# Attention and a mixture of experts on one core: half of each tile's gated row is turned by a DMA transpose instead of on TensorE

## The reference, cut to what matters

```python
x = x + _layernorm(attn(_layernorm(x), wq, wk, wv, wo))
z = _layernorm(x)
for _ in range(LOOPS):
    z_norm = rmsnorm(z, norm_w)
    scores = softmax(z_norm @ router_w)
    topk_vals, topk_idx = top_k(scores, 2)
    for e in range(E):        
        h = silu(flat_z @ w1[e]) * (flat_z @ w3[e])
        mixed = mixed + flat_cw[:, e:e + 1] * (h @ w2[e])
    z = z + mixed
x = x + _layernorm(z)
```

## Time and profile before

| what | value |
|---|---|
| median of 3 runs | 1050.5 us (1049.72 to 1050.72) |
| profiled execution, its own time | 1050.72 us |
| span of the profile (first to last instruction) | 1049.0 us |
| TensorE busy | 987.4 us (94%) |
| VectorE, ScalarE, Pool busy | 690.5, 574.7, 579.5 us |
| queue q1 (SyncE's DMAs), share of the 16 DMA engines | 26.5% |
| queue q0 (Pool's DMAs) | 12.0% |

### The profile page before, as it was taken

How to read it: one execution, slowest core, us unless ns; L and a number is a source line. 1 busy time by engine, 2 the same in 40 slices (tenths; PEclk the granted TensorE clock), 3 DMA queues, 4 the chain that set the end, 5 groups by cost and what they waited for, 6 DMA issues and landing times.

```text
span 1049.0 us, 22711 instructions
## 1 busy us (share of the span) xinstructions
PE 987.4 (94%) x7246; PEld 678.7 (65%) x7246; DVE 690.5 (66%) x1497; ACT 574.7 (55%) x1122; POOL 579.5 (55%) x755
## 2 busy tenths in 40 slices
PE   7999997989999899999999999999999999999991
PEld 5677776668888577665666765666755566666661
DVE  7889987999999454684435557535469433575557
ACT  4578786668888545433335565335574333333333
POOL 3356686866798755444443366443365544455435
PEclk9999999999999999999999999999999999999996
DMA  9921111000000234334346435338434433665573
GB/s 315 370 68 31 38 32 22 1 6 21 15 26 16 67 107 125 87 69 101 91 109 167 132 98 139 88 106 181 112 111 117 96 91 92 170 173 119 143 187 130
DMA packets 153818, 109.26 MB, mean 104 GB/s; under 512 B 100992, under 2 KB 140544, under 8 KB 153728
## 3 DMA queue, kind: packets, MB, share of 16 engines
q1 hardware_dynamic: 140096, 70.82, 26.5%
q0 software_dynamic: 13632, 37.24, 12.0%
HBM read 54.27 MB, written 31.20 MB: 81 GB/s over the span
## 4 chain that ended last, share of the span: by engine, by line
PE 69%; DVE 9%; POOL 7%; DMA 6%; ACT 4%; issue 3%; SPq 0%; another core or an unknown queue 0%; POOLq 0%; ACTq 0%; DVEq 0%
PE psum_s L930 32%; PE psum_o L2336 16%; PE psum_s L2325 6%; DMA arena<-arena 4%; PE psum_s L1758 3%; PE psum_t L1753 2%; PE psum_t L764 2%; PE psum_o L1804 2%; POOL arena L1057 2%; DVE arena L1489 1%; DMA arena<-in_rope 1%; PE psum_o L1799 1%; PE psum_o L1811 1%; PE psum_s L1735 1%; PE psum_t L2300 1%
## 5 line engine op out<-in xcount | busy, mean ns | idle before, releaser
L930 PE MATMUL psum_s<-w_all,arena 128*128 x1704 | 392.0, 380 | 4.6 <-issue 1.9
L1980 POOL DMA_INDIRECT token_rows<-arena,result_row_of_row x142 | 147.1, 1036 | 296.5 <-ACT arena L2089 291.2
L930 PEld LDWEIGHTS psum_s<-w_all,arena 128*128 128x128 f16 x1704 | 157.8, 98 | 185.2 <-issue 10.9
L2336 PE MATMUL psum_o<-w_all,arena 128*128 x1704 | 209.4, 273 | 9.1 <-DVE arena L2264 8.2
L915 DVE SCALAR_TENSOR_TENSOR arena<-psum_s,gate_scale,arena 128x512 f32<-128x512 f32 x142 | 106.5, 750 | 161.1 <-ACT arena L909 80.6
L2336 PEld LDWEIGHTS psum_o<-w_all,arena 128*128 128x128 f16 x1704 | 164.7, 98 | 54.1 <-issue 15.4
L2264 DVE TENSOR_TENSOR arena<-psum_s,arena 128x512 f16<-128x512 f32 x142 | 97.8, 689 | 132.3 <-ACT arena L2082 114.2
L2089 ACT ACTIVATE arena<-psum_o 128x256 f32<-128x256 f32 x142 | 54.3, 383 | 216.8 <-PE psum_o L2336 214.1
L891 POOL DMA_INDIRECT arena<-sorted_rows,token_of_row x142 | 139.9, 986 | 49.3 <-issue 40.2
L909 ACT ACTIVATE arena<-psum_s,silu_scale 128x512 f32<-128x512 f32 x142 | 97.6, 687 | 108.1 <-PE psum_s L930 56.6
L2082 ACT ACTIVATE arena<-psum_s 128x512 f16<-128x512 f32 x142 | 84.7, 597 | 33.1 <-PE psum_s L2325 22.9
(11 more groups left out here) (326 smaller groups left out, 1364.8 us busy)
## 6 DMA issues: line engine op xcount, KB each, us to landing
arena<-token_rows SPq DMA_DIRECT2D x64, 256.0 KB, 3.1
w_all<-in_L_ffn_w SPq DMA_DIRECT2D x24, 512.0 KB, 10.1
sorted_rows<-w_all SPq DMA_DIRECT2D x24, 256.0 KB
out<-x_sb SPq DMA_DIRECT2D x7, 512.0 KB, 3.1
arena<-arena SPq DMA_TRANSPOSE x172, 2.4
arena<-sorted_rows,token_of_row POOLq DMA_INDIRECT x142
token_rows<-arena,result_row_of_row POOLq DMA_INDIRECT x142
x_sb<-in_L_attn_x SPq DMA_DIRECT2D x1, 2048.0 KB, 14.8
```

Source lines behind the costliest of these rows:

```text
L930: last = nc.tensor.matmul(bank, e_xT[:, u, lx * DC + c, :], w_split[:, bass.ds(e * EW + at, FF)], start=(q == 0), stop=(q == 3 * DC - 1))
L1980: nc.gpsimd.indirect_dma_start(rows, bass.IndirectOffsetOnAxis(ap=targets[:, at : at + 1], axis=0), y_row[:, u, :], None).then_inc(s_sent[ ...
L2336: last = nc.tensor.matmul(psum_e, hT[:, lh, c, :], w_split[:, bass.ds(e * EW + at, D)], start=(q == 0), stop=(q == 3 * FC - 1))
```

## The change

`h_row` is gated in two halves of 256 columns, the second one first. That half is split into 16-bit hi and lo as it stands: ScalarE rounds it (`half_hi`), VectorE writes the rest (`half_lo`), into `h_split`. One DMA transpose on SyncE turns both parts of it (`turn_half`) into `hT[1]`. TensorE turns the first half in two transposes instead of four; `h_hi` and `h_lo` work on 256 columns. `outer` reads blocks 0 and 1 from `hT[0]` and then waits for the DMA before blocks 2 and 3. The buffers for results go from three to two, which frees the room for `h_split`. On SyncE `turn_half(n)` stands first in turn n, `turn_rows` goes from two tiles ahead to three, and `store_rows` comes one turn later.

```diff
             dve.wait_ge(s_b, s + 1)
             dve.wait_ge(s_silu, s + 1)
-            nc.vector.scalar_tensor_tensor(h_row, psum_b, gate_scale[:, 0:1], silu_a, ALU.mult,
-                                           ALU.mult).then_inc(s_h, 1)
+            if s:
+                dve.wait_ge(s_half_lo, s)
+            for half, signal in ((slice(FF // 2, FF), s_gated), (slice(0, FF // 2), s_h)):
+                nc.vector.scalar_tensor_tensor(h_row[:, half], psum_b[:, half], gate_scale[:, 0:1], silu_a[:, half], ALU.mult,
+                                               ALU.mult).then_inc(signal, 1)
...
+            def turn_half(n):
+
+                sp.wait_ge(s_half_lo, n + 1)
+                if n:
+                    sp.wait_ge(s_e, n)
+                sp.dma_start(hT[1].rearrange("p l c t -> p (l c) t"), h_split.rearrange("p l c -> p (l c)"),
+                             transpose=True).then_inc(s_half_T, 16)
...
-                    turn_rows(sp, FIRST[k] + t + 2)
+                    n = FIRST[k] + t
+                    turn_half(n)
+                    if n == 0:
+                        turn_rows(sp, 2)
+                    turn_rows(sp, n + 3)
...
-                    if k < END and 0 <= t - plan.split - 1 < PAIRS:
-                        store_rows(k, t - plan.split - 1)
+                    if k < END and 0 <= t - plan.split - 2 < PAIRS:
+                        store_rows(k, t - plan.split - 2)
...
+            def half_hi(n):
+                act.wait_ge(s_gated, n + 1)
+                if n:
+                    act.wait_ge(s_half_T, 16 * n)
+                nc.scalar.activation(h_split[:, 0, :], h_row[:, FF // 2 :], ACT.Copy).then_inc(s_half_hi, 1)
 
             def y_copy(n):
-                u = n % UNROLL
                 act.wait_ge(s_e, n + 1)
-                if n >= UNROLL:
-                    act.wait_ge(s_sent[u], 16 * (n // UNROLL))
-                nc.scalar.activation(y_row[:, u, :], psum_e, ACT.Copy).then_inc(s_yrow, 1)
+                if n >= 2:
+                    act.wait_ge(s_sent[(n - 2) % UNROLL], 16 * ((n - 2) // UNROLL + 1))
+                nc.scalar.activation(y_row[:, n % 2, :], psum_e, ACT.Copy).then_inc(s_yrow, 1)
...
                     if k < END:
                         beside(k, plan, t)
+                    half_hi(n)
                     if n:
                         y_copy(n - 1)
...
+            def half_lo(n):
+                dve.wait_ge(s_half_hi, n + 1)
+                nc.vector.tensor_tensor(h_split[:, 1, :], h_row[:, FF // 2 :], h_split[:, 0, :], ALU.subtract).then_inc(s_half_lo, 1)
...
                     gate(dve, n)
+                    half_lo(n)
                     if k < END:
                         beside(k, plan, t)
...
-                for c in range(FC):
+                for c in range(FC // 2):
                     last = nc.tensor.transpose(psum_h[:, c * P : (c + 1) * P], h_row[:, c * P : (c + 1) * P], ident[:, :])
...
+                    if q == 3 * FC // 2:
+                        pe.wait_ge(s_half_T, 16 * (n + 1))
```

20 lines of the change are left out of this document (13 added, 7 removed).

## The result

The changed kernel takes **1152.1 us** (median of 4 runs, 1147.6 to 1154.3), the kernel before 1050.6 in the same series: a ratio of 1.096, 95% interval 1.092 to 1.100. The forecast was 1087 us, with a range of 1062 to 1112. The sign was right, the loss was 101.5 us and not 36.5.

What follows compares the result with a forecast made beforehand. TensorE's instruction stream was taken to bound the expert stage. 1050.7 - 21.8 (transposes) + 31.6 (store loop) + 13 (large loads) + 5 (last-pass loads) + 4.7 (VectorE) + 4 (small things) = 1087.2 us; range 1062 to 1112.

Steps and rivals of the forecast that it cites:

- What it no longer has to do is worth its full price: TensorE in the expert stage: two fewer transposes save 0.22 us in each of 99 tiles, -21.8 us.
- The price per transpose: TensorE: each further transpose costs 0.11 us, as transposes overlap, though one lasts 0.27 us.
- The paragraph on quiet tiles: Undisturbed tiles: VectorE's split gating ends in time for the transposes, hidden; 0.13 us per tile if uncovered.
- Slack 0.7 us: hidden in quiet tiles: Undisturbed tiles: the half's DMA transpose lands at 3.85 us after gate, needed at 4.58, so it costs nothing.
- Rival (c): Quiet tiles: transposes meeting gathers or scatters land late, each of 99 tiles loses 0.3 us, 1117 us; chance 0.13.
- The store loop: Row stores, first three passes: half, store landing and ScalarE's row writes wait on each other in a ring; +31.6 us.
- Large loads: Before tiles 42, 73, 113 and 137: the next half's transpose stands behind four 256 KB loads; 4 x 3.3 = +13 us.
- L930's and the outer product's matmuls as long as before: Expected sign in the profile after: these TensorE matmuls keep their duration, with transposes halved to some 43 us busy.
- Loads of the last pass: Tiles 115 to 120: load pairs issued behind both transposes keep VectorE waiting, +5 us; second and third pass just fit.
- VectorE and small things: Tiles where VectorE ends last, its side work starting later, +4.7 us; several effects under 2 us each, +4 us.
- (a): Rival: the half is always in time, also behind stores and loads; faster, 1034 us; chance 0.07.
- (b): Rival: stores don't bind but large loads do; 1056 us; chance 0.08.

Runs made afterwards that it cites:

- x3_two_turns_index: The kernel before with two of four TensorE transposes per tile left out and the next expert's number loaded ahead of the transposes; 1019.5 us, ratio 0.973.
- x9_own_half: The kernel with all four edits, but TensorE reads the first half's turned data twice and never waits for the second half's DMA; 1073.9 us, ratio 1.026.
- x11_half_unread: x9_own_half with the half's DMA reading constant weights; ScalarE's wait for its landing and SyncE's for the outer product removed; 1038.5 us, ratio 0.989.
- all four edits: Changed kernel with expert number loaded before transposes, stores issued earlier, large loads spread, ScalarE's half ahead of row writes in those tiles; 1072.6 us, ratio 1.022.
- x1_index_first: The changed kernel with TensorE loading the next tile's expert number ahead of the two transposes, not behind them; 1135.7 us, ratio 1.085.

## Why the prediction was wrong, by its own steps

**"What it no longer has to do is worth its full price"**: this is the step that failed, in the first paragraph. The earlier trace rows show a tile without a gap on TensorE, and the prediction took that for proof that only matmuls bound it. A second path through the same engine's queue, gate to expert number to address to first inner matmul, was 0.01 us shorter than the path through the transposes, and its instruction stands in the trace of before. The price per transpose, 0.11 us, was right (x3_two_turns_index: 4.12 for 4.35). The paragraph on quiet tiles priced the split gate at 0.13 us per tile "if that cover were gone". The transposes keep this cover, they start 1.11 behind the gate as before; the load of the number has none, and the tile is 0.12 longer. Instead of -0.22 per quiet tile the change brings +0.12: for 64 tiles 22 of the 32 us between forecast and result; the rest are late halves and, for some 3 us, the four long loads of the expert's number.

**"Slack 0.7 us: hidden in quiet tiles"**: the median landing was right (2.46 for 2.4), the spread wasn't asked for. The prediction argued that the 2.4 is a median that holds such meetings too; a tile that waits each time pays the tail and never gets the short ones back. Rival (c) named this with 0.3 us in every tile from gathers and scatters; it is 0.5 to 1.3 us in single tiles (29, 36, 40, 68, 96, 103, 107, 110, 132, 135). The mechanism that it named is real where the meeting happens: in x9_own_half, with the scatter issued right behind the half, the quiet halves take 3.25 us. In the quiet tiles of the changed kernel the scatter is issued 0.55 us behind the half and most halves escape it. The rival's point of decision, quiet tiles over 4.3 us, was reached for another reason, the expert number.

**The store loop**: the ring and its links were right, and confirmed at two ends. The term was 31.6 us and the six turns of each stretch gave 38.4: a store's landing took 2.4 to 2.9 us, not 2.2, and gates in the second and third pass come 7.5 and 7.8 us apart on the mean, not 7.25. Tile 12 and the stretches' ends make it 41. Wrong was "TensorE waits for it in the middle of its outer product": in the second and third pass it waits in front of it, for VectorE's L2291, whose place in the queue behind the half's low part the prediction didn't follow.

**Large loads**: right in place and mechanism, 18.6 for 13. TensorE's four waits are 3.1, 2.7, 3.0 and 4.0 us, as forecast in range, but a second tile pays as well, 43 with 2.2 us, 114 with 1.4 and 138 with 1.1. In tile 43 that is TensorE's clock: the 12 inner matmuls behind the stall take 4.83 us, where they take 2.76 elsewhere (last section).

**"L930's and the outer product's matmuls as long as before"**: the prediction had no term for the clock. An inner matmul takes 389 ns on the mean and not 380, one of the outer product 279 and not 273, and the granted clock is 0.89 and 0.85 in the second and third store stretch. How much of the loss this is by itself, beside the waits that bring it about, was not separated. The transposes are busy for 57.9 us and not the "some 43", as two take 0.38 us together.

**Loads of the last pass**: right in mechanism, 9.6 for 5. The statement that in the second and third pass "this just fits" was wrong in five of sixteen tiles (46, 49, 76, 78, 81), where VectorE waits for loads that land at 4.7 us instead of 3.1 of the earlier trace rows.

**VectorE and small things**: priced at 8.7, less 7.7 of gain; these tiles cost 16.2. The first tiles alone, 0 to 5, have 4.7, for which the prediction had no term. In tile 0 the outer product waits 2.95 us in its middle for the half, which lands late there too; the rest of these tiles was not looked into.

**Sums**: two are off by little. The ring's four terms make 6.47 and not 6.45 us, the single VectorE terms 4.9 and not 4.7.

**Rivals**: (a) and (b) are excluded, since stores and loads both bind. The two y_row buffers cost nothing that shows, as said.

**The direction**: x11_half_unread and x3_two_turns_index say what was to be had. Even with all four edits and a half that nobody waits for, the change gives 12 us (7 to 17); with the lateness that a DMA has on this kernel it gives none. None of the versions with a real half beats the kernel before.

## What to carry to other kernels

A gapless engine is bound by its work only if nothing else ends level with it: before pricing what is taken off, follow the queue's own instructions (register loads, address arithmetic behind a wait) from the same starting point and see by how much they lose. A DMA that every tile waits for must be costed by its spread and not by its median alone (here 2.46 at the median and 4.0 at the ninetieth percentile, with 0.7 us of slack), and every buffer on its way is a wait of its own. Ahead of such a DMA no queue position is free: each DMA issued behind it in one tile is ahead of the next tile's, and whatever shares an engine's queue with its producer may tie it to another transfer.

## What the runs showed of the hardware

- TensorE's queue needs 0.74 us from the start of a register load (0.30 us itself) to the first matmul that is addressed by it, in most tiles of the changed kernel, and does it behind a wait only when the wait is over. The load itself took up to 1.14 us, behind a 512 KB store.
- A DMA transpose of 128 KB in a quiet tile lands 2.42 us after its issue at the median when Pool's scatter is issued 0.55 us behind it (x1_index_first), and 3.25 when it is issued 0.06 behind it (x9_own_half).
- DMA packets of 16 KB in a queue of kind instruction last 0.9 to 2.0 us each and come with TensorE's instruction stream, 43 in 700 us; 2272 register instructions fewer make them 34.
- A stall of TensorE is paid twice. In tile 58 it waits 4.9 us in front of the outer product; the granted clock falls from full speed to half (1.2 GHz) during the wait and is still there in the row from 685 to 686, with work back since 682.99, so that this outer product takes 2.74 us instead of 1.47:

```profile
679.00:680.00 1.00, 0.00 (x0) 0.00 (x0) 0.97 (x2) 0.00 (x0) 1.00 (x2) 1.00 0.87 202
...
681.00:682.00 1.00, 0.00 (x0) 0.00 (x0) 0.83 (x6) 0.00 (x0) 0.33 (x1) 0.50 0.56 177
...
685.00:686.00 1.00, 1.00 (x7) 0.81 (x6) 0.93 (x4) 0.24 (x1) 0.00 (x0) 0.50 0.00 0
```

```profile
682.99 2.74 PE L2370 MATMUL psum_o<-w_all,arena 128*128 x12 [4.91 <-DVE arena L2291]
```

Tile 43, behind the stall of the large loads (the inner product between its outer product and that of tile 42):

```profile
584.25 4.83 PE L938 MATMUL psum_s<-w_all,arena 128*128 x12
```
